# A decoder layer on one core: the seam between self attention and cross attention re-ordered, and the last three normalisations of the first phase on GpSimd

## The chip, the core and the metric

One NeuronCore of a Trainium2 chip runs the whole kernel in one launch. The metric is the device time of one execution in microseconds (us); lower is better. The engines run their own instruction streams in order and wait for each other on semaphores: TensorE (PE; its weight loads are PEld), VectorE (DVE), ScalarE (ACT), GpSimd (POOL) and SyncE (SP), which here only issues DMAs. The profiled execution is a single one.

## The reference, cut to what matters

`x` is 16 x 256 x 256, 4096 tokens of 256 features, and goes through three sublayers, each with a residual sum and a layer norm: self attention, cross attention over `ctx`, and a feed-forward part of four experts. The change lies where the first meets the second.

```python
# first sublayer: scores from a small network per head
Q, K, V = x @ wq + bq, x @ wk + bk, x @ wv + bv         # heads of 16
qp, kp = [tanh(T @ w1 + b1) @ w2 + b2 for T in (Q, K)]  # second layer: w2
qe, ke = rotate(hadamard(qp)), rotate(hadamard(kp))     # the combination
qq, kk = sum(qe ** 2), sum(ke ** 2)                     # the norms
s = qq * kk
attn = softmax(s / s)
x1 = layernorm(x + (attn @ V) @ wo + bo)
# second sublayer, 16 heads, two softmaxes
attn = softmax(q1 @ k1.T / 4) - gain * softmax(q2 @ k2.T / 4)
x2 = layernorm(x1 + headnorm(attn @ v) @ wo.T)
# third sublayer: feed-forward with routed experts
```

## The kernel before, in words

The 16 batch entries are worked on in eight pairs `p` of 512 tokens. The kernel has three phases, `phase_a`, `phase_b` and `phase_c`, each of which gives one function per engine. Nothing is scheduled by a planner: the order of every engine is written out, phase A over periods `J` and phase B over steps `s`, with functions such as `due(J, 5, 4, NIT)` that tell in which period or step an item has its turn. Each engine has one in-order queue, so all that stands behind a wait waits too.

**Phase A** (L175) runs 64 periods (`NJ`) with four first-layer products and tanh each (L426, L578), and afterwards 18 more for what is left. The query side and the key side of a pair are two of the 16 iterations `n`, four periods each. In period J, TensorE does `w2(J - 1)` (L440), the second layer into bank P[6]; VectorE moves it with its bias to EE (L699). After four of these comes `combine_pairs(n)` (L450) into P[7], its square on ScalarE (L593), and `norms(n)` (L471), again into P[7]. VectorE takes minimum and maximum of one side into KM (L721) and multiplies the other side by them into SM (L726, L727). SyncE turns SM into WS by two DMAs, VectorE makes the ratio RC in three operations (L748 to L752), ScalarE its exponential TX (L588), SyncE turns TX into TA, and TensorE multiplies by MB in `attend`, or for the last pair in two halves, `attend_last` (L492). VectorE adds the input, loaded to XM, into X1 (L624), takes statistics (L764, L769), GpSimd the root (L803, L805), and VectorE normalises four tiles of 128 tokens (L775).

**Phase B** (L828) has 256 steps. In step s TensorE does `maxima(s + 14)` (L1149), the scores whose row maxima VectorE reduces (L1423); two pairs of banks take turns, so maxima(k) wait for reduction k - 2. It then does `scores(s)` (L1169) into P[4] and P[5], which wait for the exponential of s - 1 on ScalarE (L1366), and in even steps `values` (L1182). Beside these stand, at their turns: `rows` (L1161), transposes of the negated maxima of eight steps, once in eight steps, which ScalarE moves to NR (L1330) and SyncE puts into QT (`put_maxima`, L1048), and `scores` wait for it; `turn_o` and `turn_n`; `prep_k` (L1121), three matmuls into P[7] whose result ScalarE copies (L1356), VectorE subtracts (L1441) and GpSimd copies again (L1550), for a block of keys that SyncE then loads; `prep_x` (L1129), which needs the normalised X1; and `prep_v` (L1139). The context of a pair is loaded by `load_ctx` (L1014) and split by GpSimd in four operations, `split_ctx(p, k)` (L1510), which `prep_k` waits for by the count `pool_c`; those of pair 1 also wait for the last combination, whose memory they take over.

**The seam.** The periods 58 to 81 also issue the steps -52 to 28 of phase B: `SOON_STEPS` (L162) gives the last step of each period, so J = 64 has the steps -17 to -6, 65 has -5 to -3, 66 has -2 to 1, 67 has 2 to 4, 68 has 5 to 8, 69 to 74 have 9 to 14 one by one, and then two each. Each engine's loop over J (L356, L518, L580, L693, L794) says what of phase A comes before the steps and what behind. `busy` (L1111) issues matmuls whose result nobody reads; `BUSY` (L825) says how many in which step.

The calls that the change touches are all in these loops.

```python
for j in ((J - 2,) if J < NJ else (J - 2, J - 1) if J == NJ else ()):   # L694
```

Of the kernel before, what the change touches and what calls it, by code (L numbers as in the profile page):

```python
# [9 lines left out]
NP = 8  # L10
# [154 lines left out]
FIRST_STEP, LATER_STEP = -52, 29  # L165


def soon(J):
# [6 lines left out]
def phase_a(M):  # L175
# [97 lines left out]
    pool_hi = M.sem("a_pool_hi")  # L273
    pool_rs = M.sem("a_pool_rs")
    pool_zero = M.sem("a_pool_zero")
    pool_seq = M.pool_seq
# [44 lines left out]
    def sync(e, first, step):  # L321
# [34 lines left out]
        for J in PERIODS:  # L356
# [8 lines left out]
            if p is not None:  # L365
                load_x(p + 2)
            p = due(J, 10, 8, NP)
            if p is not None:
# [19 lines left out]
    def tensor(e, first, step):  # L388
# [51 lines left out]
        def w2(j, free):  # L440
            w.wait_ge(dve_w2p, 1)
            w.wait_ge(act_th, 4 * j + 4)
            w.wait_ge(*free)
            for half in range(2):
                for k in range(4):
                    t = mm(e, P[6][32 * k:32 * k + 32, :], w2p[:, half, :], H1[(4 * j + 2 * half + k // 2) % 8][:, k % 2, :], half == 0, half == 1)
            t.then_inc(pe_w2, 1)
            return dve_ee, j + 1

        def combine_pairs(n, free):  # L450
            p = n // 2
            at, _ = CONST["sre"]
            w.wait_ge(dve_ee, 4 * n + 4)
            w.wait_ge(dve_cs, 1)
# [63 lines left out]
        for J in PERIODS:  # L518
# [46 lines left out]

    def scalar(e, first, step_b):
# [6 lines left out]
        def step(s):  # L573
# [4 lines left out]
            e.activation(H1[s % 8][:, :, :], PP[s % 3][:, :, :], ACT.Tanh, bias=b1c[:, half:half + 1], scale=1.0).then_inc(act_th, 1)  # L578

        for J in PERIODS:  # L580
# [8 lines left out]
            n = due(J, 5, 4, NIT)  # L589
            if n is not None:  # L590
                w.wait_ge(pe_qe, n + 1)
                w.wait_ge(pe_qq, n)
                e.activation(SQ[:, :], P[7][:, :], ACT.Square, bias=0.0, scale=1.0).then_inc(act_sq, 1)  # L593
            if J == SOON:
                first()
            for s in soon(J):
                step_b(s)
            for r in range(2, 4):
                if J < NJ:
                    step(4 * J + r)  # L600

    def vector(e, first, step):
# [88 lines left out]
        t.then_inc(dve_cs, 1)  # L691

        for J in PERIODS:  # L693
            for j in ((J - 2,) if J < NJ else (J - 2, J - 1) if J == NJ else ()):  # L694
                if j < 0:
                    continue
# [8 lines left out]
            if m is not None:  # L705
# [7 lines left out]
                                MV[:, :, :].unsqueeze(3).to_broadcast([128, 2, 4, 16]), ALU.mult).then_inc(dve_mm, 1)  # L713
            n = due(J, 6, 4, NIT)
            if n is not None:
                p = n // 2
                o = P[7][0:48, 0:256]
                w.wait_ge(pe_qq, n + 1)
                if n % 2 == 0:
                    w.wait_ge(dve_sm, p)  # L720
                    e.tensor_reduce(KM[:, 0:1], o, AX.X, ALU.min)  # L721
                    e.tensor_reduce(KM[:, 1:2], o, AX.X, ALU.max).then_inc(dve_km, 1)
                else:
                    w.wait_ge(dve_km, p + 1)
                    w.wait_ge(d_ws, 32 * p)
                    e.tensor_scalar(SM[:, :, 0, :], o.rearrange("q (g t) -> q g t", g=4), KM[:, 0:1], None, ALU.mult)  # L726
                    e.tensor_scalar(SM[:, :, 1, :], o.rearrange("q (g t) -> q g t", g=4), KM[:, 1:2], None, ALU.mult).then_inc(dve_sm, 1)  # L727
            m = means2_due(J)
# [15 lines left out]
            p = due(J, 11, 8, NP)  # L744
            if p is not None:
# [15 lines left out]
            if p is not None:  # L761
# [4 lines left out]
                seq.wait()  # L766
                w.wait_ge(dve_nrm, p)
# [10 lines left out]
    def gpsimd(e, first, step):  # L778
# [15 lines left out]
        for J in PERIODS:  # L794
# [4 lines left out]
            if p is not None:  # L799
                w.wait_ge(dve_ag, p + 1)  # L800
                w.wait_ge(dve_nrm, p)
                one.wait()
# [5 lines left out]
            for s in soon(J):  # L808
                step(s)

    ends = {"xs": (dve_xs, NP), "stack": [(d_st[0][c], 128 * 5) for c in range(2)], "nrm": dve_nrm, "w1": pe_w1, "w2": (pe_w2, NJ),
            "tanh": act_th, "combine": (pe_qe, NIT), "attend": (dve_x1, 2 * NP)}
# [11 lines left out]

BUSY = {-12: 2, -11: 2, -10: 1, -9: 1, -8: 1, -7: 1, -6: 1, -5: 1, -4: 1, -2: 3, -1: 1, 0: 1}  # L825


def phase_b(M, a_end):  # L828
# [176 lines left out]
    def turn_n_due(s):  # L1005
        return due(s, 23, 8, NU)

    def fold_due(s):
        return 13 if s == NS + 2 else due(s, NS - 12, 1, 13)

    def sync(e):
# [73 lines left out]
        def step(s):  # L1085
# [3 lines left out]
            if u is not None:  # L1089
                put_maxima(u)  # L1090
            p = due(s, -36, 32, NP - 1)
            if p is not None:
                load_ctx(p + 1)
            for i in range(4):
# [11 lines left out]
    def tensor(e):  # L1106
# [22 lines left out]
        def prep_x(B):  # L1129
            p, c = B // 2, B % 2  # L1130
            w.wait_ge(M.d_const, 32)
            w.wait_ge(a_end["nrm"], p + 1)
            w.wait_ge(*free[6])
# [132 lines left out]
        def step(s):  # L1266
# [3 lines left out]
            if s == 0:  # L1270
                busy(2)
            if 0 <= s < NS:
# [233 lines left out]
    def gpsimd(e):  # L1506
# [27 lines left out]
        def step(s):  # L1534
            if s == -16:
                after(w, "w2")
                clear_vt(0)
            if s == 15:
                after(w, "attend")
                clear_vt(1)  # L1540
            for k in range(4):
                p = due(s, 2 * k - (10 if s < 0 else 14), 32, NP - 1)
                if p is not None:
                    split_ctx(p + 1, k)
            k = k_due(s - 2)
# [950 lines left out]
```

## Time and profile before

| | |
|---|---|
| median of three runs | 1554.4 us |
| lowest and highest | 1553.18 and 1560.53 us |
| the profiled execution | 1558.77 us |
| its span, first to last instruction | 1557.0 us |
| mean granted TensorE clock | 0.989 |
| TensorE busy | 1507.5 us (97%) |
| VectorE busy | 1142.5 us (73%) |
| ScalarE busy | 847.5 us (54%) |
| GpSimd busy | 368.5 us (24%) |

The page divides the span into 40 equal slices of 38.9 us. Its digits are the busy share in tenths, and PEclk is the TensorE clock granted, where 9 stands for 90% or more. In the views below, times are us from the start of the span, and "ps" is a PSUM bank. A row of a timeline merges neighbouring instructions of a kind; its second number runs from the first one's start to the last one's end. TensorE's matmuls in full fp32 count as two instructions each.

### The profile page before, as it was taken

Reading aid. Unit: us, or ns where it says so; the run is one execution under the profiler, and the core shown is the slowest. Engines: PE = TensorE matmul, PEld = TensorE weight load, DVE = VectorE, ACT = ScalarE, POOL = GpSimd, SP = SyncE. Lnnn points to the kernel's source line nnn. Section 1 sums busy time; section 2 is a strip of 40 time slices with the busy share of each in tenths; the row PEclk is TensorE's granted clock in tenths of the full one; section 3 lists DMA queues with packets and bytes.
Section 4 is the critical chain, followed back from the end, with each engine's and each line's share of the span. In section 5 each row is a group of like instructions: output and inputs, shape, how many; then the busy total and the mean of one; then the engine's idle time right before and its main releaser. Section 6 shows DMA issues by size and latency. Waiting matters only on the chain.

```text
span 1557.0 us, 28838 instructions
## 1 busy us (share of the span) xinstructions
PE 1507.5 (97%) x11294; PEld 1067.9 (69%) x11294; DVE 1142.5 (73%) x2310; ACT 847.5 (54%) x1122; POOL 368.5 (24%) x400
## 2 busy tenths in 40 slices
PE   8999999898999999999999999999999999999998
PEld 4334333334566666666656898888989898888887
DVE  6445555558799999999967877777676767777675
ACT  5888889764688888888874331222222221222221
POOL 1000001123445666667453310000000000000000
PEclk9999999998899999999999999999999999999999
DMA  7656665455465675656652100000000000000000
GB/s 158 132 110 124 129 117 99 69 94 104 64 111 92 99 104 88 108 85 86 101 172 68 62 1 15 1 14 1 1 15 1 14 1 15 1 15 1 1 15 14
DMA packets 61576, 97.37 MB, mean 63 GB/s; under 512 B 12461, under 2 KB 29881, under 8 KB 61441
## 3 DMA queue, kind: packets, MB, share of 16 engines
q1 hardware_dynamic: 61312, 95.34, 33.1%
q8 instruction: 89, 1.46, 0.4%
q14 instruction: 47, 0.38, 0.1%
q10 hardware_dynamic: 128, 0.20, 0.0%
HBM read 26.29 MB, written 4.19 MB: 20 GB/s over the span
## 4 chain that ended last, share of the span: by engine, by line
PE 86%; DVE 8%; ACT 2%; issue 2%; SPq 2%; DMA 0%; POOL 0%; POOLq 0%; DVEq 0%; ACTq 0%
PE ps L109 81%; PE ps L1203 2%; SPq L119 2%; DVE NM L1423 1%; ACT PX L1366 1%; DVE EE L699 1%; ACT H L578 1%; PE ps L1165 1%; PE ps L1211 1%; DVE XC L2034 1%; PE ps L1842 0%; PE ps L1833 0%; DVE X L775 0%; PE ps L1135 0%; DVE X L624 0%
## 5 line engine op out<-in xcount | busy, mean ns | idle before, releaser
L1423 DVE TENSOR_REDUCE NM<-ps 128x4 f32<-128x1024 f32 x256 | 307.7, 1220 | 34.5 <-PE ps L109 32.9
L1366 ACT ACTIVATE PX<-ps 128x1024 f32<-128x1024 f32 x256 | 262.4, 1025 | 83.0 <-PE ps L109 81.7
L578 ACT ACTIVATE H<-ps,b1c 128x1024 f32<-128x1024 f32 x256 | 268.4, 1120 | 47.1 <-PE ps L109 45.5
L1994 ACT ACTIVATE GF<-ps,cols 128x512 f32<-128x512 f32 x128 | 88.2, 689 | 295.7 <-PE ps L109 295.5
L109 PE MATMUL ps<-XC,W_sw_w 128*128 128x512 f32 x768 | 185.7, 392 | 0.0
L2185 DVE CAST GH<-GF 128x512 fp32r<-128x512 f32 x192 | 82.1, 427 | 106.9 <-ACT GF L1994 101.8
L109 PEld LDWEIGHTS ps<-XC,W_sw_w 128*128 128x128 f32 x768 | 140.5, 188 | 27.9
L2293 POOL TENSOR_SCALAR RSc<-AGc 128x4 f32<-128x4 f32 x23 | 6.9, 301 | 599.5 <-DVE AGc L2080 599.5
L109 PE MATMUL ps<-PX,VT 128*32 128x256 f32 x2048 | 140.0, 392 | 0.1
L2187 DVE TENSOR_TENSOR GH<-GF,GH 128x512 fp32r<-128x512 f32 x192 | 133.2, 694 | 6.6
L109 PE MATMUL ps<-KT,QT 48*128 48x512 f32 x512 | 129.4, 502 | 2.0 <-DVE NM L1423 1.9
L1989 ACT ACTIVATE GF<-ps 128x512 f32<-128x512 f32 x64 | 38.1, 597 | 169.2 <-PE ps L109 169.2
L109 PE MATMUL ps<-H,w2p 128*32 128x512 f32 x1024 | 124.8, 606 | 4.0 <-ACT XF L1335 1.1
L109 PE MATMUL ps<-QT,KT 52*128 52x256 f32 x1024 | 111.1, 294 | 6.0 <-ACT PX L1366 5.1
L109 PEld LDWEIGHTS ps<-QT,KT 52*128 52x128 f32 x1024 | 91.7, 190 | 28.0 <-ACT PX L1366 12.7
L699 DVE TENSOR_SCALAR EE<-ps,b2p 128x512 f32<-128x512 f32 x64 | 47.8, 747 | 77.9 <-PE ps L109 77.8
L109 PE MATMUL ps<-W_ml_w,GH 128*128 128x256 f32 x768 | 103.6, 285 | 0.2
L109 PEld LDWEIGHTS ps<-W_sw_w,GH 128*128 128x128 f32 x768 | 100.0, 191 | 4.5
L109 PEld LDWEIGHTS ps<-KT,QT 48*128 48x128 f32 x512 | 48.4, 186 | 79.5 <-issue 62.2
L109 PE MATMUL ps<-W_sw_w,GH 128*128 128x256 f32 x768 | 102.7, 283 | 0.0
L109 PEld LDWEIGHTS ps<-W_ml_w,GH 128*128 128x128 f32 x768 | 98.0, 191 | 5.8 <-issue 3.4
L109 PE MATMUL ps<-ST,w1s 48*128 48x512 f32 x512 | 96.6, 451 | 5.0 <-ACT H L578 2.0
(238 smaller groups left out, 2560.0 us busy)
## 6 DMA issues: line engine op xcount, KB each, us to landing
KT<-KS SPq DMA_DIRECT2D x128, 192.0 KB, 4.7
ST<-QS SPq DMA_DIRECT2D x254, 96.0 KB, 2.8
QT<-XSb SPq DMA_DIRECT2D x128, 96.0 KB, 4.1
XT<-in_xT_dram SPq DMA_DIRECT2D x8, 512.0 KB, 4.5
raw_a<-in_x_dram SPq DMA_DIRECT2D x8, 512.0 KB, 4.3
CR<-in_ctxT_dram SPq DMA_DIRECT2D x8, 512.0 KB, 4.5
out_dram<-X SPq DMA_DIRECT2D x7, 512.0 KB, 3.0
R_sw_w<-in_sw_w_dram SPq DMA_DIRECT2D x6, 512.0 KB, 5.8
```

The lines of the kernel that those rows point to most:

```text
L109: return e.matmul(o, l, r, start=start, stop=stop, skip_group_check=True)
L119: e.dma_start(o, i).then_inc(sem, 16)
L578: e.activation(H1[s % 8][:, :, :], PP[s % 3][:, :, :], ACT.Tanh, bias=b1c[:, half:half + 1], scale=1.0).then_inc(act_th, 1)
L699: e.tensor_scalar(EE[:, j % 4, :], P[6][:, :], b2p[:, 0:1], None, ALU.add).then_inc(dve_ee, 1)
L1165: t = e.transpose(low[0:32, 128 * qc:128 * qc + 128], f32(NS2[u % 2][:, 4 * qc:4 * qc + 4, :, :]).rearrange("p g l n -> p (g l n)"), ident)
L1203: t = e.transpose(P[7][:, 256 * qc + 128 * i:256 * qc + 128 * i + 128], OT[f][:, i, 128 * qc:128 * qc + 128], ident)
L1366: e.activation(PX[s % 3][:, :, :, :], PP[2][:, :, :].rearrange("p g (c q) -> p g c q", c=2), ACT.Exp, bias=0.0, scale=0.25).then_inc(act_e ...
L1423: e.tensor_reduce(NM[u % 2][:, qc, :, :, i], PP[qc][:, :, :].rearrange("p g (m k) -> p g m k", m=2), AX.X, ALU.max, negate=True).then_inc( ...
L1989: e.activation(g[:, :], o, ACT.Silu, bias=0.0, scale=1.0).then_inc(act_g, 1)
L1994: e.activation(g[:, :], o, f, bias=cols[:, col:col + 1], scale=1.0).then_inc(act_g, 1)
L2185: e.tensor_copy(h[:, 0, :], g[:, :]).then_inc(dve_h, 1)
L2187: e.tensor_tensor(h[:, 1, :], g[:, :], f32(h[:, 0, :]), ALU.subtract).then_inc(dve_h, 1)
```

## The change

- The second layer of period 63 is issued behind the steps' s = -13, that is behind the first two maxima, instead of ahead of all steps of J = 64; ScalarE instead of VectorE makes its EE.
- The last combination stands behind the steps of J = 65 (before: ahead of them), the last norms behind those of J = 66, and VectorE's last products as well.
- The WS transfers, the ratio and the exponential of the last pair come one period later, the two `attend_last` in J = 72 and 74 (before 70 and 74).
- GpSimd normalises the pairs 5, 6 and 7, at the end of the periods 65, 73 and 81.
- In phase B, `prep_k` of block 2, first half, moves from s = -5 to 0; the load of context 2 from s = -4 to 5; the four splits of context 1 from s = -10, -8, -6, -4 to -4, -2, 0, 2; `clear_vt(1)` from 15 to 17.
- Of 20 matmuls of `busy`, 6 are left.

```diff
+LAST_W2 = -13
...
+    def ws_due(J):
+        return NP - 1 if J == NJ + 3 else due(J, 10, 8, NP - 1)
+    def ratio_due(J):
+        return NP - 1 if J == NJ + 4 else due(J, 11, 8, NP - 1)
     def exp_due(J):
-        return NP - 1 if J == NJ + 5 else due(J, 12, 8, NP - 1)
+        return NP - 1 if J == NJ + 6 else due(J, 12, 8, NP - 1)
     def last_due(J):
-        return due(J, NJ + 6, 4, 2)
+        return due(J, NJ + 8, 2, 2)
+    POOL_NORM = 5
+    def normalised(p):
+        return (dve_nrm, p + 1) if p < POOL_NORM else (pool_nrm, p - POOL_NORM + 1)
...
 tensor:
-            n = due(J, 5, 4, NIT)
+            n = due(J, 5, 4, NIT - 1)
-            n = due(J, 6, 4, NIT)
+            n = due(J, 6, 4, NIT - 1)
-            if 1 <= J <= NJ:
+            if 1 <= J < NJ:
                 free[6] = w2(J - 1, free[6])
             if J >= NJ:
                 for s in soon(J):
                     step(s)
+                    if s == LAST_W2:
+                        free[6] = w2(NJ - 1, free[6])
+            if J == NJ + 1:
+                free[7] = combine_pairs(NIT - 1, free[7])
+            if J == NJ + 2:
+                free[7] = norms(NIT - 1, free[7])
...
 scalar:
             for s in soon(J):
                 step_b(s)
+                if s == LAST_W2:
+                    w.wait_ge(pe_w2, NJ)
+                    w.wait_ge(pe_qe, NIT - 1)
+                    e.activation(EE[:, 3, :], P[6][:, :], ACT.Identity, bias=b2p[:, 0:1], scale=1.0).then_inc(act_ee, 1)
+            if J == NJ + 1:
+                square(NIT - 1)
...
 vector:
             for s in soon(J):
                 step(s)
+            if J == NJ + 2:
+                products(NIT - 1)
...
-            p = due(J, 25, 8, NP)
+            p = due(J, 25, 8, POOL_NORM)
...
 gpsimd:
             for s in soon(J):
                 step(s)
+            p = due(J, 25, 8, NP)
+            if p is not None and p >= POOL_NORM:
+                for v in range(4):
+                    one.wait()
+                    one.done(e.tensor_scalar(X1[:, 4 * p + v, :], X1[:, 4 * p + v, :], AG[:, v, 0:1], RS[:, v:v + 1], ALU.subtract, ALU.mult),
+                             pool_nrm if v == 3 else pool_seq)
...
-BUSY = {-12: 2, -11: 2, -10: 1, -9: 1, -8: 1, -7: 1, -6: 1, -5: 1, -4: 1, -2: 3, -1: 1, 0: 1}
+BUSY = {-10: 1, -9: 1, -8: 1, -7: 1, -6: 1}
...
     def k_due(s):
-            if B is not None:
+            if B is not None and (B, m) != (2, 0):
                 return B, m
-        return None
+        return (2, 0) if s == 0 else None
+    def ctx_due(s):
+        return 2 if s == 5 else 1 if s == -36 else s // 32 + 3 if s in range(28, 28 + 32 * (NP - 3), 32) else None
+    def split_due(s, k):
+        return 1 if s == 2 * k - 4 else s // 32 + 2 if s in range(2 * k + 18, 2 * k + 18 + 32 * (NP - 2), 32) else None
...
             if s == 0:
-                busy(2)
+                busy(1)
-            if s == -5:
-                busy(2)
-            if s == 15:
+            if s == 17:
                 after(w, "attend")
                 clear_vt(1)
```

## Rows read from the trace of the kernel before

**Rows 1.** The page, part 2: TensorE's granted clock in 40 slices.
```profile
PEclk9999999998899999999999999999999999999999
```

**Rows 2.** Windows: length, busy us (instructions) by engine, clock, DMA share, GB/s.
```profile
366.00:373.00 7.00, 5.90 (x36) 3.42 (x37) 3.86 (x5) 3.70 (x5) 0.00 (x0) 0.53 0.80 119
...
386.00:393.00 7.00, 6.21 (x25) 3.94 (x29) 4.14 (x7) 1.94 (x5) 2.55 (x4) 0.56 0.46 70
...
400.00:410.00 10.00, 9.04 (x59) 5.02 (x60) 6.42 (x10) 4.83 (x6) 8.38 (x8) 0.52 0.69 102
```

**Rows 3.** Windows from one transpose of row maxima to the next, eight steps each.
```profile
372.07:389.90 17.83, 15.81 (x136) 9.51 (x135) 15.26 (x28) 11.47 (x16) 5.13 (x7) 0.88 0.55 103
389.90:409.98 20.08, 18.64 (x132) 10.38 (x131) 14.22 (x22) 11.25 (x15) 9.12 (x9) 0.67 0.63 92
409.98:425.67 15.69, 14.57 (x143) 9.48 (x144) 13.86 (x26) 12.78 (x19) 7.91 (x9) 0.98 0.15 18
425.67:439.70 14.03, 13.34 (x140) 8.88 (x141) 13.45 (x21) 12.12 (x18) 7.69 (x9) 1.00 0.84 153
```

**Rows 4.** Timeline of VectorE: start, us, engine, line, operation, [idle before <- releaser].
```profile
342.63 3.48 DVE L1423 TENSOR_REDUCE NM<-ps 128x4 f32<-128x1024 f32 x3
...
346.62 5.74 DVE L1423 TENSOR_REDUCE NM<-ps 128x4 f32<-128x1024 f32 x5
...
357.06 1.23 DVE L1423 TENSOR_REDUCE NM<-ps 128x4 f32<-128x1024 f32 x1 [1.75 <-PE ps L109]
...
359.94 1.79 DVE L775 TENSOR_SCALAR X<-X,AG,RS 128x256 f32<-128x256 f32 x4
361.65 0.47 DVE L726 TENSOR_SCALAR SM<-ps,KM 48x256 f32<-48x256 f32 x1
...
362.43 4.60 DVE L1423 TENSOR_REDUCE NM<-ps 128x4 f32<-128x1024 f32 x4
```

**Rows 5.** Timeline of TensorE, the same columns.
```profile
339.98 1.92 PE L109 MATMUL ps<-H,w2p 128*32 128x512 f32 x16 [0.97 <-DVE EE L699]
...
345.51 0.89 PE L109 MATMUL ps<-bdv,CH 128*128 128x128 f32 x6
...
352.12 1.06 PE L109 MATMUL ps<-EE,C 128*32 128x512 f32 x8
...
355.40 1.20 PE L109 MATMUL ps<-CH,G 128*128 128x512 f32 x4 [0.56 <-POOL CH L1521]
...
359.03 0.61 PE L109 MATMUL ps<-SQ,C 128*16 128x256 f32 x4 [0.96 <-DVE KS L1441]
...
367.01 0.63 PE L109 MATMUL ps<-KT,QT 48*128 48x512 f32 x2
...
386.79 1.99 PE L109 MATMUL ps<-MB,TA 32*128 32x256 f32 x4 [1.32 <-DVE PR L1417]
```

**Rows 6.** Timeline of ScalarE: the last tanh, and the first later table load.
```profile
337.58 2.13 ACT L578 ACTIVATE H<-ps,b1c 128x1024 f32<-128x1024 f32 x2
...
838.05 1.28 ACT L1989 ACT_TABLE_LOAD   x1
```

**Rows 7.** Timeline of SyncE's queue, DMA issues.
```profile
360.22 0.38 SPq L119 DMA_DIRECT2D CR<-in_ctxT_dram  x1
...
364.90 1.66 SPq L119 DMA_DIRECT2D WS<-SM  x2
366.60 0.60 SPq L119 DMA_DIRECT2D KT<-KS  x1
...
375.67 1.44 SPq L119 DMA_DIRECT2D QT<-NR  x2
```

**Rows 8.** Three lines of the kernel over the span: ns least/median/most, first and last start.
```profile
L1592 POOL TENSOR_SCALAR X<-X,AGb,RSb x32: 1222/1232/2527, 496.9 to 895.6; 128x256 f32<-128x256 f32 x32
...
L775 DVE TENSOR_SCALAR X<-X,AG,RS x32: 399/406/831, 144.1 to 430.4; 128x256 f32<-128x256 f32 x32
...
L1521 POOL TENSOR_TENSOR CH<-CR,CH x16: 1271/1286/1547, 300.5 to 704.2; 128x512 fp32r<-128x512 f32 x16
```

More of the change, by code:

```diff
@@ L274, in phase_a @@
     pool_rs = M.sem("a_pool_rs")
+    pool_nrm = M.sem("a_pool_nrm")
+    act_ee = M.sem("a_act_ee")
     pool_zero = M.sem("a_pool_zero")
@@ L366, in sync @@
                 load_x(p + 2)
-            p = due(J, 10, 8, NP)
+            p = ws_due(J)
             if p is not None:
@@ L447, in w2 @@
             t.then_inc(pe_w2, 1)
-            return dve_ee, j + 1
+            return (dve_ee, j + 1) if j < NJ - 1 else (act_ee, 1)
         def combine_pairs(n, free):
@@ L452, in combine_pairs @@
             at, _ = CONST["sre"]
-            w.wait_ge(dve_ee, 4 * n + 4)
+            w.wait_ge(dve_ee, min(4 * n + 4, NJ - 1))
+            w.wait_ge(act_ee, n - NIT + 2)
             w.wait_ge(dve_cs, 1)
@@ L578, in step, with square @@
             e.activation(H1[s % 8][:, :, :], PP[s % 3][:, :, :], ACT.Tanh, bias=b1c[:, half:half + 1], scale=1.0).then_inc(act_th, 1)
+        def square(n):
+            w.wait_ge(pe_qe, n + 1)
+            w.wait_ge(pe_qq, n)
+            e.activation(SQ[:, :], P[7][:, :], ACT.Square, bias=0.0, scale=1.0).then_inc(act_sq, 1)
         for J in PERIODS:
@@ L588, in scalar @@
                 e.activation(TX[:, :], RC[:, 0, :], ACT.Exp, bias=0.0, scale=1.0).then_inc(act_tx, 1)
-            n = due(J, 5, 4, NIT)
+            n = due(J, 5, 4, NIT - 1)
             if n is not None:
-                w.wait_ge(pe_qe, n + 1)
-                w.wait_ge(pe_qq, n)
-                e.activation(SQ[:, :], P[7][:, :], ACT.Square, bias=0.0, scale=1.0).then_inc(act_sq, 1)
+                square(n)
             if J == SOON:
@@ L691, in vector, with extremes, products @@
         t.then_inc(dve_cs, 1)
+        low = P[7][0:48, 0:256]
+        def extremes(n):
+            w.wait_ge(pe_qq, n + 1)
+            w.wait_ge(dve_sm, n // 2)
+            e.tensor_reduce(KM[:, 0:1], low, AX.X, ALU.min)
+            e.tensor_reduce(KM[:, 1:2], low, AX.X, ALU.max).then_inc(dve_km, 1)
+        def products(n):
+            w.wait_ge(pe_qq, n + 1)
+            w.wait_ge(dve_km, n // 2 + 1)
+            w.wait_ge(d_ws, 32 * (n // 2))
+            e.tensor_scalar(SM[:, :, 0, :], low.rearrange("q (g t) -> q g t", g=4), KM[:, 0:1], None, ALU.mult)
+            e.tensor_scalar(SM[:, :, 1, :], low.rearrange("q (g t) -> q g t", g=4), KM[:, 1:2], None, ALU.mult).then_inc(dve_sm, 1)
         for J in PERIODS:
-            for j in ((J - 2,) if J < NJ else (J - 2, J - 1) if J == NJ else ()):
-                if j < 0:
-                    continue
+            j = J - 2
+            if 0 <= j <= NJ - 2:
                 w.wait_ge(pe_w2, j + 1)
@@ L713, in vector @@
                                 MV[:, :, :].unsqueeze(3).to_broadcast([128, 2, 4, 16]), ALU.mult).then_inc(dve_mm, 1)
-            n = due(J, 6, 4, NIT)
+            n = due(J, 6, 4, NIT - 1)
             if n is not None:
-                p = n // 2
-                o = P[7][0:48, 0:256]
-                w.wait_ge(pe_qq, n + 1)
                 if n % 2 == 0:
-                    w.wait_ge(dve_sm, p)
-                    e.tensor_reduce(KM[:, 0:1], o, AX.X, ALU.min)
-                    e.tensor_reduce(KM[:, 1:2], o, AX.X, ALU.max).then_inc(dve_km, 1)
-                else:
[L724 to L727, printed above, removed]
+                    extremes(n)
+                else:
+                    products(n)
             m = means2_due(J)
@@ L743, in vector @@
                 attended(NP - 1, u, 7)
-            p = due(J, 11, 8, NP)
+            p = ratio_due(J)
             if p is not None:
@@ L766, in vector @@
                 seq.wait()
-                w.wait_ge(dve_nrm, p)
+                if p:
+                    w.wait_ge(*normalised(p - 1))
                 for v in range(4):
@@ L800, in gpsimd @@
                 w.wait_ge(dve_ag, p + 1)
-                w.wait_ge(dve_nrm, p)
+                w.wait_ge(dve_nrm, min(p, POOL_NORM))
                 one.wait()
@@ L809, in gpsimd @@
                 step(s)
-    ends = {"xs": (dve_xs, NP), "stack": [(d_st[0][c], 128 * 5) for c in range(2)], "nrm": dve_nrm, "w1": pe_w1, "w2": (pe_w2, NJ),
+            p = due(J, 25, 8, NP)
[4 more added lines that the diff above has]
+                             pool_nrm if v == 3 else pool_seq)
+    ends = {"xs": (dve_xs, NP), "stack": [(d_st[0][c], 128 * 5) for c in range(2)], "nrm": normalised, "w1": pe_w1, "w2": (pe_w2, NJ),
             "tanh": act_th, "combine": (pe_qe, NIT), "attend": (dve_x1, 2 * NP)}
@@ L1090, in step @@
                 put_maxima(u)
-            p = due(s, -36, 32, NP - 1)
+            p = ctx_due(s)
             if p is not None:
-                load_ctx(p + 1)
+                load_ctx(p)
             for i in range(4):
@@ L1131, in prep_x @@
             w.wait_ge(M.d_const, 32)
-            w.wait_ge(a_end["nrm"], p + 1)
+            w.wait_ge(*a_end["nrm"](p))
             w.wait_ge(*free[6])
@@ L1541, in step @@
             for k in range(4):
-                p = due(s, 2 * k - (10 if s < 0 else 14), 32, NP - 1)
+                p = split_due(s, k)
                 if p is not None:
-                    split_ctx(p + 1, k)
+                    split_ctx(p, k)
             k = k_due(s - 2)
```

## The prediction

> **What bounds the kernel now.** I read the page's forty slices first. TensorE has work nearly everywhere, and its granted clock dips in one place, the tenth and eleventh slice [rows 1], where the first phase (self attention, periods J up to 64) meets the second (cross attention, steps s). In windows of that seam the clock is at the lower of its two levels (1.2 of 2.4 GHz) most of 366 to 373, 386 to 393 and 400 to 410 us [rows 2]. The transposes of the row maxima come once in eight steps, so they are milestones: at 372.07 (s = 3), 389.90, 409.98, 425.67 and 439.70 us. Eight steps take 17.83, 20.08, 15.69 and then 14.03 us [rows 3]; the last is the normal pace, and the three before are over it by 3.80, 6.05 and 1.66, together 11.5 us. The second of them has a mean clock of 0.67 over 20.08 us, so 13.2 us at the lower level, and loses 6.05: a lower-clock microsecond in which TensorE has work costs about 0.46 us. That is my price for the clock.
>
> Before s = 3 the limit is VectorE. Fourteen steps of maxima run ahead of the first scores, each a reduction spaced 1.15 us. The timelines of VectorE and TensorE show what else stands in that chain: the last EE, directly ahead of the first reduction at 342.63; a wait of 1.75 us before 357.06; four normalisations at 359.94; the two products of SM at 361.65, until the reductions go on at 362.43 [rows 4]. TensorE's own waits there are for GpSimd (0.56 us, after the split of the context that ended the gap) and 0.96 us for a VectorE copy of K, ahead of the norms [rows 5].
>
> **The change part by part.** Steps are summed against the profiled execution, 1558.8 us (span 1557.0 and 1.8 around it); the median of the three runs is 4.4 lower, and I carry the difference over to it.
>
> Part 1, the last second layer. Now w2(63) starts at 339.98 because it waits for EE(62), lasts 1.92, and the first maxima come behind it [rows 5]. The last tanh ends at 339.71 (337.58 and 2.13) [rows 6], so maxima(0) can start at 339.8 and the first reduction at 340.25: 2.4 us earlier. But the K product of s = -13 (three matmuls, some 0.65 with what overlaps) and w2(63) then stand between maxima(1) and maxima(2), until 343.0, and VectorE waits 0.8. ScalarE makes the last EE in 0.60 ahead of the K copy, which VectorE takes up at 344.5, just when its third reduction ends. The fourth reduction starts at 345.1; it started at 346.62 (the three, then the K subtraction). **1.5 us gained.** What the unseen form of ScalarE costs: between 0, as the other copies there, and two table loads of 1.28 us, as where the function changes later on [rows 6]. I take 0, since Exp, Copy and Square alternate here with no load. Such loads would fall into the reduction chain and cost at most 2.6 less the cover of 1.1 that one reduction gives. The Trainium skill, "ScalarE: Activation LUTs", section "Table sets: the hidden batching unit", has identity in every set as filler, so by it the cost is 0 too; no row here shows that function on ScalarE.
>
> Part 2, the stretch to the first scores. Out of VectorE's chain go the four normalisations of pair 5 (1.71, from 359.94 to 361.65), the products (0.78, moved behind the reduction of s = 1), the wait of 1.75 with another of 0.15, and the K subtraction (0.60), whose prep_k moves from s = -5 to s = 0 [rows 4]: 5.0 us. Reduction 14 starts at 364.73 now (two after 362.43), so it would start at 358.2, and scores(0) follow at about 358.0 instead of 364.8. **6.5 us gained so far.** SyncE covers it: the context load that held it until 360.22 [rows 7] moves to s = 5. The put of the first maxima would be issued at 352, and scores(0) leave it six.
>
> Part 3, GpSimd's queue, the step on which I rest most. The K product of block 2 at s = 0 needs the first two of the four context splits. The first now stands at s = -4 (J = 65), the second at s = -2 (J = 66), and the normalisation of pair 5 is issued **between them**, at the end of J = 65. All of it waits for the last combination, moved behind maxima(11) and a V product (six matmuls, 0.89 less what overlaps with the next) [rows 5]: maxima(11) at 353.9, then 0.7 and 1.06 give 355.6, where it ended at 353.2. From there GpSimd needs 0.70 (first split with its spacing), four normalisations of 1.23 at a spacing of 1.31 (5.2), and 1.36 for the second split [rows 8]: 7.3 us, so 363.05. TensorE, done with scores(0) at 358.4, executes in order and waits **4.7 us** before the K product; behind it queue maxima(15), scores(1), the norms and so all of VectorE and ScalarE. Maxima(15) come at 363.7, its reduction at 364.1; it started at 365.88. **Of the 6.5 gained, 1.8 are left.** VectorE does such a normalisation in 0.41, so GpSimd takes 3.0 times as long [rows 8]. By the Trainium skill, "GPSIMD Engine Reference", section "Key points", VectorE is about twice as fast in elementwise work; by it the four would take 3.2 and the wait would be 3.0. The row decides, 4.7.
>
> Part 4, norms and products. The norms write the bank that the K product has just filled, so they wait for its copy by ScalarE and the subtraction by VectorE, which is behind the reduction of s = 1 (364.1, then 1.15, then 0.60). Norms at 365.9 to 366.5, products until 367.3, maxima(16) at 366.5; now it is 367.01 [rows 5]. **0.5 left.** The lower-clock stretch, now 366 to 373 with TensorE at work in 5.9 of 7 us [rows 2], I expect to begin in the wait of part 3, where half of it hits nothing: 3.4 us by 0.46 gives 1.6. **2.1.**
>
> Part 5, SyncE. The WS transfers leave after the products, at 367.4 rather than 364.90, then come XM and the fourth load of block 1, and only then the second put of maxima, issued now at 375.67, for which scores(8) wait [rows 7]. Between 364.90 and 375.67 now lies a third load as well (3.5 us, 366.60 to 370.08 in that timeline), which in the changed kernel is issued while SyncE waits for the products. So the chain is 10.8 less 3.5, 7.3 us long, and the put leaves at 374.7: 1.0 us earlier. Of the 2.1 I count **1.0** at s = 8.
>
> Part 6, the attend steps. attend_last(0) waits 1.32 us for VectorE now, and the clock falls during it [rows 5, 2]. It moves from s = 10 to 12, where its bank is held by the K product of s = 11, so it waits for that subtraction, behind the reduction of its own step: again about 1.2. The ratio (1.45 us of VectorE) moves from behind s = 4 to behind s = 8, close to the statistics of pair 6: no gain, no loss in sum. The normalisation of pair 6 (1.37) leaves VectorE ahead of the second attend: **1.3** gained; 0 if VectorE is not last there. Two attends two steps apart instead of four bring the two falls of the clock together; I take one lower stretch of 14.5 us for two of 17, **1.1**. Pair 7 leaves VectorE where eight steps take 14.03 anyway: 0, covered by TensorE. On GpSimd it delays an output norm that has eight steps of slack.
>
> Part 7, fourteen fill matmuls fewer of twenty. Where TensorE waits for VectorE they cost nothing, so removing them gives 0. The loss is in the clock, as a rival.
>
> Sum: 1.0 + 1.3 + 1.1 = **3.4 us**; 1558.8 gives 1555.4, the median 1554.4 gives **1551.0**. Chance of this case, 0.48, with 1547 to 1554 as its own range.
>
> **The rivals.** A measurement of this kernel tells about 0.5% (7.8 us) from no change.
>
> A, the clock holds. For it: the moved w2, combination and norms are real work where fills were, and most of the 11.5 us over the normal pace hangs on the clock. Against it: the wait of 4.7. If two of the three lower stretches go (3.8 and 3.0 after s = 3) and GpSimd is ready 3 us sooner, the gain is about 10: 1544.4. Chance 0.22.
>
> B, slower, at one place: s = -5 to -3. There the fills are gone and the combination comes later, so TensorE has three maxima in 4 us and little more. If the clock falls there, at 350 to 355 us, the V product and the combination take about 1.8 us longer, maxima(12) is late by 2, GpSimd starts 2 later and K(2,0) comes at 365; by part 4 TensorE is then 1.5 to 3 behind the present kernel and part 6 returns half. It decides when the granted clock is below 1 before scores(0). Net 2.5 us slower: 1556.9. Chance 0.22; in 0.06 of it the lower clock lasts to s = 19 as well and the loss is above 7.8.
>
> C, SyncE's chain hides all: if the second put comes no earlier than 375.67, the gain up to s = 8 is 0, the waits of the attends stay, and it is 1553.6. The change then only moves the wait. Chance 0.08.
>
> **How the numbers follow.** Faster by over 0.5% (under 1546.6): most of A, 0.19, and the edge of the first case, 0.03: 0.22. Slower by over 0.5% (over 1562.2): 0.06. Within: 0.72. The range takes A's value less 1 and B's value with a table load, 1543.0 to 1559.5; some 0.08 lies below and 0.11 above.
>
> **What would show it.** The first reduction should start within 0.6 us of the end of EE(62), and the EE on ScalarE take 0.60 with no table load. Between the two GpSimd splits stand four normalisations of 1.23; TensorE waits 4 to 5 us for the split ahead of the K product of s = 0. The norms wait for the K subtraction. The eight steps from s = 11 to 19 stay over 16 us. I am wrong if TensorE does not wait for the split, if scores(0) come later than 360, or if the clock is at full level from scores(0) on.

## The result: slower by 0.46%, outside the range

| | before | after |
|---|---|---|
| median of 11 runs each | 1554.74 us | 1563.06 us |
| lowest to highest | 1552.41 to 1560.53 | 1560.93 to 1565.25 |
| profiled execution / its span | 1558.8 / 1557.0 | 1561.24 / 1559.4 |
| mean granted clock of that execution | 0.989 | 0.986 |

The ratio is 1.0046 with an interval of 1.0033 to 1.0059, so about 7.2 us slower (the two medians are 8.3 apart). The prediction was 1551.0 with a range of 1543.0 to 1559.5: wrong in sign and outside the range, though inside the half per cent that it called no change. The two profiled executions differ by only 2.5 us, because the one of before was 4 us above its own median. That matters for everything below.

The page of the changed kernel, parts 1 and 2 (of the clock row, the dip is where it was in [rows 1], and deeper):

```profile
PE 1504.9 (97%) x11280; PEld 1066.1 (68%) x11280; DVE 1139.1 (73%) x2297; ACT 848.0 (54%) x1123; POOL 383.2 (25%) x412
...
PEclk9999999997899999999999999999999999999999
```

Windows of the seam, changed kernel (length, busy us by engine with instructions, clock, DMA share, GB/s), then the four stretches of eight steps that answer to [rows 3]:

```profile
338.00:352.00 14.00, 12.01 (x70) 5.42 (x62) 11.65 (x14) 4.09 (x7) 5.35 (x7) 1.00 0.54 73
352.00:362.00 10.00, 8.23 (x36) 4.05 (x35) 7.31 (x7) 2.14 (x5) 3.46 (x4) 0.66 0.53 72
362.00:376.00 14.00, 8.41 (x44) 4.49 (x45) 5.27 (x9) 3.99 (x6) 5.82 (x6) 0.51 0.38 59
...
375.53:389.16 13.63, 13.21 (x131) 7.82 (x130) 12.31 (x18) 11.57 (x16) 3.12 (x4) 0.98 0.60 134
389.16:412.51 23.35, 19.70 (x134) 11.15 (x134) 16.28 (x27) 11.26 (x15) 14.15 (x15) 0.71 0.67 96
412.51:428.16 15.65, 14.03 (x144) 9.28 (x145) 14.81 (x27) 12.66 (x19) 9.79 (x11) 1.00 0.15 18
428.16:441.94 13.78, 13.56 (x139) 8.87 (x140) 12.37 (x18) 12.12 (x18) 12.26 (x12) 1.00 0.83 151
```

The milestone s = 3 is at 375.53 and was at 372.07, with the last tanh ending 0.16 earlier: 3.6 us are lost in the seam itself, while the clock is at the lower level from 352.1 to 358.9 and again from 362.3 to 376.0. Then 13.63 instead of 17.83 gives 4.2 back, and 23.35 instead of 20.08 loses 3.3 of it. The rest is alike: 2.4 us at s = 35, which is the difference of the two executions.

TensorE in the seam, its timeline:

```profile
352.77 0.80 PE L109 MATMUL ps<-KT,QT 48*128 48x512 f32 x2 [0.74 <-DVE NM L1476]
...
354.62 1.54 PE L109 MATMUL ps<-bdv,CH 128*128 128x128 f32 x6
356.10 1.94 PE L109 MATMUL ps<-EE,C 128*32 128x512 f32 x8
...
360.95 0.50 PE L109 MATMUL ps<-QT,KT 52*128 52x256 f32 x4
365.56 1.65 PE L109 MATMUL ps<-CH,G 128*128 128x512 f32 x3 [4.11 <-POOL CH L1574]
...
370.39 1.04 PE L109 MATMUL ps<-SQ,C 128*16 128x256 f32 x4 [2.03 <-DVE KS L1494]
371.36 0.79 PE L109 MATMUL ps<-KT,QT 48*128 48x512 f32 x2
```

GpSimd's, over the same time:

```profile
358.22 0.62 POOL L1572 CAST CH<-CR 128x512 fp32r<-128x512 f32 x1 [7.13 <-PE ps L109]
358.95 5.21 POOL L855 TENSOR_SCALAR X<-X,AG,RS 128x256 f32<-128x256 f32 x4
364.24 1.26 POOL L1574 TENSOR_TENSOR CH<-CR,CH 128x512 fp32r<-128x512 f32 x1
```

And VectorE's:

```profile
340.24 2.36 DVE L1476 TENSOR_REDUCE NM<-ps 128x4 f32<-128x1024 f32 x2 [0.56 <-PE ps L109]
343.65 1.23 DVE L1476 TENSOR_REDUCE NM<-ps 128x4 f32<-128x1024 f32 x1 [1.06 <-PE ps L109]
...
345.39 5.74 DVE L1476 TENSOR_REDUCE NM<-ps 128x4 f32<-128x1024 f32 x5
...
358.80 3.49 DVE L1476 TENSOR_REDUCE NM<-ps 128x4 f32<-128x1024 f32 x3 [2.69 <-PE ps L109]
367.98 1.23 DVE L1476 TENSOR_REDUCE NM<-ps 128x4 f32<-128x1024 f32 x1 [5.68 <-PE ps L109]
```

Read the three together. The clock falls at 352.1, the V product takes 1.54 instead of 0.89 [rows 5] and the combination 1.94 instead of 1.06, so it ends at 358.03. GpSimd, which has waited 7.13 us for it, makes the first split, four normalisations, and only then the second split, to 365.50. TensorE stands for 4.11 us. VectorE, starved behind it, is idle for 5.68.

### The profile page after: what moved, and what is told of

It is laid out like the page before. It is cut to its first block, busy times and chain, and to the rows that moved or that the text cites. A ratio compares the mean times of both kernels' runs of the same rounds, so it can differ in the third digit from the quotient of the medians.

```text
span 1559.4 us, 28810 instructions
## 1 busy us (share of the span) xinstructions
PE 1504.9 (97%) x11280; PEld 1066.1 (68%) x11280; DVE 1139.1 (73%) x2297; ACT 848.0 (54%) x1123; POOL 383.2 (25%) x412
## 4 chain that ended last, share of the span: by engine, by line
PE 86%; DVE 7%; ACT 3%; issue 2%; SPq 2%; POOL 0%; DMA 0%; POOLq 0%; DVEq 0%; ACTq 0%
PE ps L109 81%; PE ps L1258 2%; SPq L119 2%; DVE NM L1476 1%; ACT PX L1419 1%; ACT H L601 1%; DVE EE L745 1%; PE ps L1220 1%; PE ps L1266 1%; DVE XC L2087 1%; PE ps L1895 0%; PE ps L1190 0%; PE ps L1886 0%; DVE X L656 0%; POOL X L855 0%
```

## The experiments

Each was compared with runs of the kernel before beside it, 32 or 35 in a session. Two columns come from the one profiled execution of each kernel: from the end of the last tanh to the transposes of s = 3 (the seam), and from there to s = 27 (24 steps).

| kernel | median us | ratio [95%] | clock, median of runs | seam | 24 steps |
|---|---|---|---|---|---|
| before | 1554.74 | 1 | not on record (beside the experiments: 0.990 to 0.991) | 32.4 | 53.6 |
| after | 1563.06 | 1.0046 [1.0033, 1.0059] | 0.984 | 36.0 | 52.6 |
| e1_fills | 1561.24 | 1.0032 [1.0019, 1.0045] | 0.986 | 32.9 | 51.6 |
| e2_norm_late | 1559.83 | 1.0025 [1.0014, 1.0036] | 0.985 | 33.2 | 53.2 |
| e3_fills_late | 1557.15 | 1.0004 [0.9992, 1.0016] | 0.990 | 30.5 | 51.7 |
| e4_dve_norms | 1560.02 | 1.0030 [1.0019, 1.0042] | 0.984 | 33.2 | 52.5 |
| b1_before_again | 1553.29 | 0.9996 [0.9977, 1.0014] | 0.9935 | 31.9 | 46.4 |
| e5_norms_early | 1553.09 | 0.9978 [0.9964, 0.9993] | 0.993 | 27.1 | 55.7 |
| e6_w2_alone | 1557.62 | 1.0009 [0.9996, 1.0022] | 0.989 | 33.4 | 54.1 |
| e7_attends_back | 1551.07 | 0.9965 [0.9950, 0.9980] | 0.993 | 27.1 | 50.8 |
| e8_dve_norm5 | 1550.79 | 0.9963 [0.9943, 0.9983] | 0.994 | 38.6 | 45.9 |
| e9_early_no_fills | 1553.08 | 0.9976 [0.9957, 0.9995] | 0.9885 | 31.8 | 51.9 |
| e10_w2_with_fills | 1558.67 | 1.0008 [0.9990, 1.0027] | 0.989 | 30.9 | 53.9 |
| e11_change_attends_back | 1557.91 | 1.0014 [0.9999, 1.0029] | 0.987 | 36.0 | 46.1 |

### Fills back, and the norm behind the splits

e1_fills puts the fill matmuls of s = -5 and later back, ten of the fourteen (the expectation says 11); the four of s = -12 and -11 stay out (the busy(1) stands at s = 0):

```
-BUSY = {-10: 1, -9: 1, -8: 1, -7: 1, -6: 1}
+BUSY = {-10: 1, -9: 1, -8: 1, -7: 1, -6: 1, -5: 1, -4: 1, -2: 3, -1: 1, 0: 1}
...
-                busy(1)
+                busy(2)
+            if s == -5:
+                busy(2)
```

> The changed kernel with the fill matmuls of s = -5 to 0 put back (11 of the 14 that went; the four at s = -12 and -11 stay out). Theory Q (queue): the loss is GpSimd's four normalisations ahead of the second context split; the fills do nothing, TensorE waits about 4 us for the split and the median stays at 1563 within 1.5. Theory C (clock): the loss begins where the clock falls at 352 us, before scores(0); with the fills it stays at full level there, the last combination ends at about 355.6 instead of 358.0, everything behind is 2.4 us earlier and the median is 1559 to 1561. If both hold, the wait for the split is still 4 us or more, only earlier.

e2_norm_late leaves the fills out and sends GpSimd's normalisation of pair 5 behind all four splits:

```
-            p = due(J, 25, 8, NP)
+            p = 5 if J == NJ + 3 else due(J, 25, 8, NP) if J != NJ + 1 else None
```

> The changed kernel with the normalisation of pair 5 issued by GpSimd at the end of J = 67, behind all four splits of context 1, and nothing else moved. Theory Q: the wait of 4.1 us ahead of the K product of s = 0 is gone or under 1 us, the products of SM end 4 to 5 us earlier, and the median falls by 3 to 5, to 1558 to 1560. Theory C alone: the clock still falls at 352, TensorE still comes to the K product late, and the median falls by less than 1.5.

e3_fills_late has both edits.

> Both edits: fills of s = -5 to 0 back and the normalisation of pair 5 behind the splits. If the two losses are separate and add up, this is 5.5 to 7.5 us below the changed kernel, 1555.5 to 1557.5, that is no better than the kernel before; if the order of the seam itself is a gain of some 6 us, as the blind forecast had it up to scores(0), it is below the kernel before: 1548 to 1552. If the third lower stretch of the clock, that of the attends, decides, it stays above 1558.

Timelines of TensorE, first e1_fills, then e3_fills_late:

```profile
356.22 0.89 PE L109 MATMUL ps<-bdv,CH 128*128 128x128 f32 x6
357.03 1.06 PE L109 MATMUL ps<-EE,C 128*32 128x512 f32 x8
...
365.63 0.97 PE L109 MATMUL ps<-CH,G 128*128 128x512 f32 x3 [2.73 <-POOL CH L1576]
```

```profile
352.16 0.95 PE L109 MATMUL ps<-CH,G 128*128 128x512 f32 x3
...
355.41 1.06 PE L109 MATMUL ps<-EE,C 128*32 128x512 f32 x8
...
365.18 1.04 PE L109 MATMUL ps<-SQ,C 128*16 128x256 f32 x4 [2.28 <-DVE KS L1496]
```

With the fills, the first of them directly behind the transposes, the clock is full until 366.6 and 365.0, and the V product and the combination cost 0.89 and 1.06 again. With the norm behind the splits TensorE's wait for GpSimd is gone and the wait for the K subtraction is what is left, 2.28. In the seam the fills give 3.0 us, the late norm 2.8 and both 5.5. In the medians it is 2.2, 3.3 and 6.5 (each is the ratio's distance from 1.0046, times 1555). The interval of both together is clear of the change's; that of each alone overlaps it. Each can also be read on top of the other: the late norm on top of the fills is worth 4.4 (1.0032 to 1.0004, intervals apart), the fills on top of the late norm 3.3 (1.0025 to 1.0004, intervals that just overlap). TensorE's wait for the split in e1_fills is 2.73, not the 4 or more expected.

e4_dve_norms gives the normalisations of pairs 5 and later back to VectorE (`POOL_NORM = 8` for 5), without the fills.

> The changed kernel with the normalisations of pairs 5, 6 and 7 back on VectorE. Theory Q: the wait for the second split goes, as in the late variant, but VectorE gets 1.7 us of work ahead of the reduction of s = -2 and 1.4 behind s = 13: 1559.5 to 1561.5. Theory C alone: VectorE, not TensorE, sets the pace at s = -3 and -2, where the combination takes its time at the lower clock, so the 1.7 us hide behind it and the median is unchanged within 1.5.

1.0030, 2.5 us better than the change with an interval that overlaps the change's: TensorE's wait for the split is gone, and the seam is as long as that of e2_norm_late, 33.2 us. So two ways of clearing the place between the splits give the same: what costs is where the work stands in GpSimd's queue. The pair e7_attends_back and e8_dve_norm5, below, bears this out for pair 5.

### The kernel before, profiled again

> The kernel before, once more with a profile, to see how much of its seam is fixed. If the lower-clock stretches belong to the program, the three of the first profile (366 to 373, 387 to 394, 401 to 411 us) come back in the same steps and the profiled time is near 1558.8. If they depend on the execution, this profile has fewer or shorter ones and a time nearer to the median of 1555.7, and the first profile was a slow sample on which the price of 0.46 us per lower-clock microsecond was charged to gains that the median never had.

Windows of eight steps, as [rows 3], of this execution of the same program:

```profile
372.23:388.18 15.95, 13.90 (x136) 8.35 (x134) 14.80 (x27) 11.27 (x16) 5.13 (x7) 1.00 0.56 110
388.18:403.27 15.09, 13.45 (x132) 7.79 (x131) 13.91 (x23) 11.12 (x15) 6.73 (x7) 1.00 0.74 104
403.27:418.65 15.38, 14.23 (x143) 9.26 (x144) 14.07 (x26) 12.65 (x19) 10.23 (x12) 1.00 0.34 43
418.65:432.68 14.03, 13.36 (x139) 8.88 (x140) 13.44 (x21) 12.11 (x18) 7.69 (x9) 1.00 0.85 159
```

The stretches from 386 to 393 and from 400 to 410 [rows 2] are not there. The second window is 15.09 long where it was 20.08, and the execution took 1553.1 instead of 1558.8. Two of the three stretches on which the prediction built its gains are not a property of the kernel but of the execution. Over the 35 runs of before beside it, the mean clock lies between 0.986 and 0.995, and 0.001 of it goes with 0.96 us (the slope of a line through them). The change has 0.981 to 0.986 in all its 11 runs. From the median 0.991 to 0.984 that slope makes 6.7 us, nearly the whole loss. But it is a correlation within one kernel and does not carry over to another: e2_norm_late is 3.3 us faster than the change at a median clock of 0.985, and e9_early_no_fills, below, is faster than before at 0.9885. How much of the loss is the clock and how much are waits is not shown by it.

### Norms and products early

e5_norms_early is e3_fills_late with the last norms and SM products directly behind s = -1, ahead of the K product that overwrites their bank:

```
+                    if s == -1:
+                        free[7] = norms(NIT - 1, free[7])
-            if J == NJ + 2:
-                free[7] = norms(NIT - 1, free[7])
-            if J == NJ + 2:
-                products(NIT - 1)
+                if s == -1:
+                    products(NIT - 1)
```

> The variant with the fills back and the normalisation of pair 5 behind the splits, and now also the last norms and the products of SM directly behind the steps' s = -1, ahead of the K product of s = 0, whose bank they share. Theory N: the norms' wait for the copy of K (2.3 us) falls away and the products end some 8 us earlier; 1.5 to 3 us below the variant before it (1557.2), so 1554 to 1556. Rival: TensorE is by then held by the maxima and the exponentials, and the wait only moves to the K product, which now needs the products' end: within 1 us of 1557.2.

Timelines of TensorE, then VectorE:

```profile
356.87 0.89 PE L109 MATMUL ps<-bdv,CH 128*128 128x128 f32 x6
357.68 0.61 PE L109 MATMUL ps<-SQ,C 128*16 128x256 f32 x4
...
359.75 0.51 PE L109 MATMUL ps<-QT,KT 52*128 52x256 f32 x4
```

```profile
356.11 2.36 DVE L1478 TENSOR_REDUCE NM<-ps 128x4 f32<-128x1024 f32 x2 [1.47 <-PE ps L109]
358.38 0.47 DVE L737 TENSOR_SCALAR SM<-ps,KM 48x256 f32<-48x256 f32 x1
358.78 0.47 DVE L738 TENSOR_SCALAR SM<-ps,KM 48x256 f32<-48x256 f32 x1
```

The norms wait for nothing, the clock, which fell in that wait in e3_fills_late, stays at its upper level to 382.0, the seam is 27.1 us (3.4 shorter), and the ratio is 0.9978: about 4 us better than e3_fills_late, though the intervals still touch. Its window from s = 11 to 19, where the attend steps are:

```profile
379.19:405.20 26.01, 23.97 (x133) 13.07 (x134) 17.19 (x27) 11.25 (x15) 15.79 (x16) 0.55 0.61 86
```

26.01 us at a clock of 0.55. That asked for the next run.

### The attend steps

e7_attends_back is e5_norms_early with ratio, exponential and last attends (in this order in the diff) at the periods of the kernel before:

```
-        return NP - 1 if J == NJ + 4 else due(J, 11, 8, NP - 1)
+        return NP - 1 if J == NJ + 3 else due(J, 11, 8, NP - 1)
-        return NP - 1 if J == NJ + 6 else due(J, 12, 8, NP - 1)
+        return NP - 1 if J == NJ + 5 else due(J, 12, 8, NP - 1)
-        return due(J, NJ + 8, 2, 2)
+        return due(J, NJ + 6, 4, 2)
```

> The variant with the early norms, and the ratio, the exponential and the two attends of the last pair in the periods of the kernel before (67, 69, 70 and 74). If moving the attends together cost time (one long stretch of lower clock, VectorE loaded by ratio and statistics at once), this is 1 to 3 us below the variant with early norms. If it is as part 6 of the forecast said, it is 1 us above it.

e11_change_attends_back is the change with this edit and nothing else.

> The changed kernel with one thing undone: ratio, exponential and the two attends in the periods of the kernel before (67, 69, 70 and 74). With the early norms this edit was worth 2.0 us. If that term is independent of the rest, 1561 against 1563.1. If the late products (at 372 us) then hold the ratio in J = 67 and with it VectorE, it is no better or worse: 1563 to 1565.

Windows of eight steps of e11_change_attends_back, against those of the changed kernel at the top:

```profile
377.45:393.59 16.14, 14.11 (x136) 8.48 (x134) 14.78 (x27) 11.44 (x16) 5.14 (x7) 0.98 0.57 121
393.59:408.15 14.56, 13.36 (x132) 7.78 (x131) 12.62 (x19) 11.14 (x15) 10.32 (x9) 1.00 0.79 117
408.15:423.54 15.39, 14.28 (x143) 9.28 (x144) 14.05 (x26) 12.66 (x19) 11.60 (x14) 1.00 0.36 46
```

The seam is the same to 0.1 us, 36.0, and the two kernels differ in nothing but the periods of ratio, exponential and attends. Within the change these are worth 5.0 us of median, where about 2 were expected (1.0014 against 1.0046, the intervals apart), and the 24 steps 6.5 in the two profiles. On top of e5_norms_early they are worth 2.0 (0.9965 against 0.9978, intervals overlapping). What happens there stands in TensorE's timeline of the changed kernel:

```profile
390.87 0.92 PE L109 MATMUL ps<-CH,G 128*128 128x512 f32 x3 [1.33 <-DVE PR L1470]
...
394.86 1.10 PE L109 MATMUL ps<-MB,TA 32*128 32x256 f32 x4 [1.21 <-DVE KS L1494]
...
396.83 1.08 PE L1258 MATMUL ps<-C,OT 128*128 128x128 f32 x4 [0.19 <-DVE X L656]
...
400.86 2.07 PE L109 MATMUL ps<-MB,TA 32*128 32x256 f32 x4
...
405.29 0.79 PE L109 MATMUL ps<-QT,KT 52*128 52x256 f32 x4 [0.79 <-ACT PX L1419]
```

The old wait for PR, 1.33, did not go away. It moved ahead of the K product, and the first attend waits another 1.21 for the K subtraction, 4 us later. The clock falls at 396.5, and the second attend, at 400.86, costs 2.07 instead of 1.1. With the attends back the waits of that stretch are 1.33, ahead of the first attend, and 0.97, 11 us behind it, and the clock does not fall there:

```profile
391.89 1.10 PE L109 MATMUL ps<-MB,TA 32*128 32x256 f32 x4 [1.33 <-DVE PR L1470]
...
402.67 0.50 PE L109 MATMUL ps<-QT,KT 52*128 52x256 f32 x4 [0.97 <-ACT PX L1419]
```

That is one execution. In the profile of e7_attends_back, with the same periods, the clock does fall there, twice, for 10.2 us in all, against 23.9 in e5_norms_early. That two waits close together bring the fall is argued from these rows. What is shown is the time of the pair of kernels.

### w2(63) alone

e6_w2_alone is the kernel before with w2(63) behind s = -13, the last EE on ScalarE, and the fills of s = -12 and -11 out (the diff of the change for those lines, nothing else). e10_w2_with_fills keeps these fills.

> The kernel before with one part of the change alone: w2(63) behind s = -13 and its EE on ScalarE (and the four fills of s = -12 and -11, whose place it takes, left out). By part 1 of the forecast the fourth reduction comes 1.5 us nearer to the last tanh and, since VectorE sets the pace from there to the first scores, the end too: 1553.5 to 1554.5 against 1555.7. Rival: the median gain is under 0.5 us, because the wait for GpSimd's splits at s = -5 takes what comes early.

> The second layer alone moved, as in the run that gave 1557.6 against 1555.0, but with the four fills of s = -12 and -11 kept. Theory C: those four, not w2 itself, cost what was lost (the clock fell at 347.5 us in that profile); with them the clock holds to the first scores and the median is 1553 to 1555, at or below the kernel before. Rival: w2 between maxima(1) and maxima(2) is itself the loss; it stays at 1557 or above, the four fills adding 0.4 us ahead of maxima(2).

Timelines of ScalarE and then TensorE in e6_w2_alone:

```profile
343.38 0.69 ACT L607 ACTIVATE EE<-ps,b2p 128x512 f32<-128x512 f32 x1 [3.70 <-PE ps L109]
343.96 0.59 ACT L1364 ACTIVATE KS<-ps 128x512 fp32r<-128x512 f32 x1
```

```profile
353.35 1.93 PE L109 MATMUL ps<-EE,C 128*32 128x512 f32 x8
...
361.39 0.61 PE L109 MATMUL ps<-SQ,C 128*16 128x256 f32 x4 [0.96 <-DVE KS L1449]
```

Ratios 1.0009 and 1.0008, both intervals over 1. Counted from the end of the last tanh, the reduction behind the first K subtraction starts 6.91 us later in before, 5.84 in e6 and 6.50 in e10, where VectorE waits 1.72 for its third reduction instead of 1.06. So the move gains 1.1 at that place without the fills and 0.4 with them. In e6's profile the clock falls at 347.5, the combination takes 1.93 and scores(0) come 2.3 later than before (27.3 against 25.1 after the tanh). In e10's it does not, and the 0.4 stays 0.4. Neither is more than the measurement tells from nothing. Both expectations of a gain (1553.5 to 1554.5 and 1553 to 1555) missed, at 1557.62 and 1558.67: the clock held up to the first scores in e10, and there was no gain either.

### The best arrangement, with one thing changed

e8_dve_norm5 is e7_attends_back with pair 5 normalised by VectorE (`POOL_NORM = 6`). e9_early_no_fills is e7_attends_back with the change's few fills.

> The best variant so far (fills back, splits ahead of the normalisation, early norms, attends in their old periods; 1551.1), with the normalisation of pair 5 back on VectorE in J = 65 and only pairs 6 and 7 on GpSimd. Theory V: VectorE sets the pace up to the first scores, so its 1.7 us come back in full: 1552.5 to 1553.5. Rival: TensorE has its combination and the V product there, and VectorE waits for it anyway: unchanged within 0.7.

> The same best variant with only the six fills of the change (none from s = -5 on but one at s = 0). Theory C: without fills the clock falls between 349 and 356 us there too, and 2 to 4 us are lost: 1553 to 1555. Rival: with the queue of GpSimd in order, TensorE is not held long, the clock recovers before the scores and the fills are worth under 1 us.

0.9963 and 0.9965 cannot be told apart: once GpSimd's normalisation of pair 5 stands behind the splits, no difference is measured between the two engines. Without the fills it is 0.9976, 1.7 us more with overlapping intervals, so the fills are not shown to pay here, though the median clock of the runs is 0.9885 against 0.993. That this lower clock falls in part into TensorE's waits would explain it, and is not shown.

e8's profile shows what a single execution is worth. Its timeline of TensorE, where the transposes of X at 347.42 take 1.00 (0.66 at the upper clock, as at 348.32 in before), and the windows behind it:

```profile
347.42 1.00 PE L1190 MATMUL ps<-C,X 128*128 128x128 f32 x4
...
352.00:362.00 10.00, 10.00 (x33) 4.92 (x33) 6.75 (x11) 1.20 (x3) 0.32 (x1) 0.50 0.45 62
362.00:379.00 17.00, 16.31 (x68) 8.49 (x67) 8.60 (x11) 5.34 (x9) 4.05 (x5) 0.52 0.61 116
```

With the fills of e1_fills in place the clock was at the lower level from 347.6 to 378.3 and the seam took 38.6 us, the longest of all. That execution took 1557.0, and the other eleven of the same kernel 1545.2 to 1556.9.

e7_attends_back and e8_dve_norm5 beat both kernels: 0.9965 and 0.9963 of the time of before, 5.4 and 5.8 us faster, and 12 to 13 us faster than the change.

## Why the prediction was wrong, by its own steps

**Part 1 held in place, not in size.** The first reduction starts at 340.24 (340.25 forecast), 0.57 after the end of EE(62), and the EE on ScalarE takes 0.69 with no table load (0.60 forecast). By the Trainium skill, "ScalarE: Activation LUTs", section "Table sets: the hidden batching unit", identity is in every set; the trace now agrees. VectorE's wait for w2 is 1.06 (0.8 forecast), the gain 1.1 counted from the tanh (1.5 forecast), and alone it does not reach the end.

**Part 2 was mis-sized.** Scores(0) come at 360.95 (358.0 forecast), 3.7 us earlier from the tanh than before, not 6.5. Even at full clock, in e3_fills_late, it is 4.1. The step summed what leaves VectorE's chain and did not ask whether TensorE could still feed it. V product, combination and fills stand between the maxima, and VectorE waits 2.69 behind them in the change and 1.47 in e5_norms_early.

**Part 3 held.** Four normalisations of 5.21 in all stand between the splits (5.2 forecast), and TensorE waits 4.11 (4.7 forecast). By the Trainium skill, "GPSIMD Engine Reference", section "Key points", VectorE is about twice as fast; the trace does not agree: 1.30 us for each here, 0.41 on VectorE in [rows 8]. The start was wrong: the combination ended at 358.03, not 355.6, so the K product came at 365.56, not 363.1.

**Part 4, where the sign turned.** Its order was right (the norms wait 2.03 for the K subtraction), its sum was not: maxima(16) at 371.36 where 366.5 was forecast and 367.01 was before. "0.5 left" was 4.35 lost, and the lower clock did not spend half of itself in the wait: two stretches, 20.5 us in all, lie over the seam, and TensorE was at work in 14.3 of them, where the forecast had one of seven with half of it harmless. Scores(0) at 360.95 were also one of the prediction's own signs of being wrong ("later than 360").

**Part 5** made no difference. The second put leaves at 378.03 (374.7 forecast), later than before, but s = 3 to 11 takes 13.63, so the chain of SyncE did not bind.

**Part 6 failed in sign.** The wait of 1.21 at attend_last(0) and one lower stretch of 13.6 us (14.5 forecast) came true. But "for two of 17, 1.1" took as given two stretches that the second profiled execution of before does not have. Forecast 1.1 gained by bringing them together; measured 5.0 lost by the move, in the change. The 1.3 for the normalisation of pair 6 was not measured by itself.

**Part 7, the step that failed first.** "Removing them gives 0. The loss is in the clock, as a rival" priced the fills at nothing in the main case. The rival B had the mechanism, the place and the order: clock lower at 350 to 355, V product and combination 1.8 longer (0.65 and 0.88 are 1.5), GpSimd 2 later, K product at 365. Its sign, a clock below 1 before scores(0), came too. It had a chance of 0.22 and a price of 2.5 us. e1_fills puts the share of ten of the fills at 2.2, with an interval that overlaps the change's; on top of the late norm they are 3.3. What it lacked was the loss at the attends, and a gain of part 4 that was never there. So two terms failed in sign, the fills at 0 for a loss of 2 to 3 us and the attends at a gain of 1.1 for a loss of 5.0, and the 4.7 us wait of part 3, foreseen and accepted, cost 3.3 to 4.4 of median. These overlap and are not a sum: together they are more than the 7.2 lost.

**The base.** The sum was made against an execution of 1558.8 us, and its gains on the clock (1.6 in part 4, 1.1 in part 6) were charged to stretches that b1_before_again shows to come and go. They could not be carried over to a median 4.4 lower: a profile above its median by that much already holds the loss that the change is meant to remove. The price of a lower-clock microsecond was high as well. Its window took 15.09 at the upper clock in b1_before_again and 20.08 in the first profile, so 13.2 us at the lower level cost 5.0, or 0.38 each and not 0.46. Three slips in the working change nothing: 355.6 and 7.3 make 362.9, not 363.05; the wait by the page's factor is 2.7, not 3.0; and A's value less 1 is 1543.4, not 1543.0.

What stays open: why the clock falls in one execution and not in another of the same program, how the 5.0 us of the attends divide between the two waits, and what the normalisations of pairs 6 and 7 are worth on VectorE by themselves (e4_dve_norms moves them together with pair 5).

## What to carry to other kernels

Cheap filler on TensorE is part of the kernel when its granted clock is near falling. Price its removal as if it were work, by what the matmuls behind it cost at the lower level, and take it out in a run of its own: here it was worth 2 to 3 us in the order of the change, and nothing that could be shown in the best one. When work moves to a slow engine, look where in that engine's queue it lands: the same four normalisations held TensorE for 4.11 us between two splits and cost about 4 us of median there (e1_fills against e3_fills_late); behind them no cost was measured (e7_attends_back against e8_dve_norm5). And where an execution differs from its median by more than the effect looked for, profile it again before charging a gain to anything that it shows.

## What the runs showed of the hardware

The granted clock at the same place of the same program is not the same from one execution to the next: over 35 runs of before its mean was 0.986 to 0.995 and the time 1551.7 to 1560.5. It can fall with TensorE busy: in e8_dve_norm5 it fell at 347.6, with TensorE at work in 6.18 of the 7.0 us ahead and waits of no more than 0.59 and 0.24 us in the last four. An ACTIVATE with the function Identity over 128x512 from PSUM takes 0.69 us, the Copy of that size next to it 0.59, with no table load between them.
